# Attention cores: the causal triangle stands in the position bias, not in a matmul of its own

## The reference

```python
sim = jnp.einsum('bhid,bjd->bhij', q, k)            # k: null key, then 1024 keys
bias = jnp.concatenate([null_col, attn_bias], axis=-1)   # attn_bias: [16, 1024, 1024]
sim = sim + bias
neg = -jnp.finfo(sim.dtype).max
causal_mask = jnp.triu(jnp.ones((n, j), dtype=bool), k=j - n + 1)
sim = jnp.where(causal_mask, neg, sim)
sim = jnp.where(mask_p[:, None, None, :], sim, neg)
attn = jax.nn.softmax(sim, axis=-1)
out = jnp.einsum('bhij,bjd->bhid', attn, v)
```

## Time and profile before

| | us |
|---|---|
| median of three runs | 3015.57 |
| span of the profiled execution, first to last instruction | 3060.8 |
| layer 0 attention core (first PE score to the last normalised output) | about 140 to 655 |
| layer 2 attention core | about 1547 to 2069 |
| PE busy, of the span | 2511.8 (82%) |
| DVE busy | 1576.5 (52%) |
| ACT busy | 1325.9 (43%) |
| POOL busy | 938.2 (31%) |

### The profile page before, as it was taken

The page is one execution under the profiler, slowest core; times in us unless marked ns, Lnnn a source line. Parts: engine busy times, 40 slices in busy tenths (PEclk is TensorE's granted clock), DMA queues, the critical chain, the costliest instruction groups (busy, mean ns, idle before and its releaser), DMA issues. The chain is left out here.

```text
span 3060.8 us, 56027 instructions
## 1 busy us (share of the span) xinstructions
PE 2511.8 (82%) x16472; PEld 2054.1 (67%) x16472; DVE 1576.5 (52%) x4371; ACT 1325.9 (43%) x3147; POOL 938.2 (31%) x1172
## 2 busy tenths in 40 slices
PE   5799999988796762995789999998599997673795
PEld 3477777767686752982467777777477786672785
DVE  3366666644214345116766666654588885425111
ACT  2365666653221331333456666664344442152221
POOL 0132333311104454544333333322333430445002
PEclk9999999998897875997989999999799998895898
DMA  7022122202564353521022122210200001144585
GB/s 267 31 78 77 64 86 70 82 27 101 197 230 110 99 193 124 173 65 52 22 85 71 63 86 70 82 42 16 80 1 1 0 0 57 65 157 158 211 307 178
DMA packets 150858, 296.59 MB, mean 97 GB/s; under 512 B 25158, under 2 KB 110406, under 8 KB 144560
## 3 DMA queue, kind: packets, MB, share of 16 engines
q1 hardware_dynamic: 138416, 262.92, 25.5%
q0 software_dynamic: 12288, 31.83, 3.4%
HBM read 240.25 MB, written 64.56 MB: 100 GB/s over the span
## 5 line engine op out<-in xcount | busy, mean ns | idle before, releaser
L796 DVE CUSTOM_DVE_ANT_0 prob_l<-ps_l,bias_l,nsn 128x1024 f32<-128x1024 f32 (+3 forms) x256 | 276.7, 1081 | 112.7 <-DVEq L795 65.4
L796 DVE CUSTOM_DVE_ANT_0 cur_sb<-ps_h,bias_s,nsn 128x128 f32<-128x128 f32 (+3 forms) x256 | 139.7, 546 | 241.7 <-DVEq L795 241.2
L871 ACT ACTIVATE prob_l<-prob_l,nmax 128x1024 f32<-128x1024 f32 (+3 forms) x256 | 252.1, 985 | 1.9 <-DVE nmax L796 1.6
L691 POOL COPY nsn<-nsn 128x4 f32 (+1 forms) x128 | 23.9, 187 | 710.7 <-DVE diff L813 570.5
L727 PE MATMUL ps_l<-khi,stage 128*128 128x512 f32 (+3 forms) x512 | 240.7, 470 | 0.0
L733 PE MATMUL ps_pt<-ident_sb,prob_l 128*128 128x128 f32 x1664 | 231.8, 276 | 5.3 <-ACT cur_sb L855 2.3
L855 ACT ACTIVATE cur_sb<-ps_pt 128x128 f32<-128x128 f32 (+3 forms) x256 | 111.1, 434 | 267.4 <-PE ps_pt L733 267.3
L700 POOL TENSOR_TENSOR stage<-qo,stage 64x256 fp32r<-64x256 f32 x256 | 200.9, 785 | 46.5 <-POOLq L699 46.5
L733 PEld LDWEIGHTS ps_pt<-ident_sb,prob_l 128*128 128x128 f32 x1664 | 186.6, 141 | 29.6 <-ACT cur_sb L855 13.9
L284 PE MATMUL ps_q<-wf,xnT 128*128 128x512 f32 (+1 forms) x384 | 148.2, 539 | 65.5 <-ACT xnT L321 53.5
L2270 POOL TENSOR_TENSOR ss<-simx,sim 128x4096 f32<-128x4096 f32 x16 | 113.4, 7084 | 239.4 <-DVE simx L2419 239.4
(11 more groups left out here) (341 smaller groups left out, 6275.8 us busy)
## 6 DMA issues: line engine op xcount, KB each, us to landing
mlp_ws<-in_L_ffn_experts_dram SPq DMA_DIRECT2D x39, 2052.0 KB, 7.5
xs<-slot_rows SPq DMA_DIRECT2D x156, 128.0 KB, 2.1
slot_outputs<-ys SPq DMA_DIRECT2D x156, 128.0 KB, 1.9
slot_rows<-zero_sb SPq DMA_DIRECT2D x1, 16384.0 KB, 51.9
bias_l<-in_fside_16xSxS_dram SPq DMA_DIRECT2D x16, 512.0 KB, 3.9
mlp_w<-in_L_ffn_experts_dram SPq DMA_DIRECT2D x8, 1024.0 KB
bias_by_partition<-bias_table SPq DMA_DIRECT2D x16, 512.0 KB, 4.2
bias_l<-bias_by_partition SPq DMA_DIRECT2D x16, 512.0 KB, 3.3
```

Source lines behind the costliest of these rows:

```text
L796: dve.tensor_tensor_reduce(out=spans(x, prob), in0=scored(x), in1=spans(x, bias), scale=-1.0, scalar=nsn[:, b, s, h:h + 1], op0=ALU.add, o ...
L871: act.activation(prob[x.s][:, x.h, 0:x.W], prob[x.s][:, x.h, 0:x.W], ACT.Exp, bias=nmax[:, x.b, x.s, x.h:x.h + 1], scale=-1.0, accum_out=r ...
```

## The change

In layer 0 POOL writes -1e38 above the diagonal of the bias tile itself, once it has landed: one `affine_select` of 128x128 for each tile that is loaded (128 of them), in place, and DVE waits for POOL's step instead of the landing. In layer 2 nothing is added: the tail of the table holds -1e38 in place of 0. The mask matmul of every unit is then one, from `km`, over all of its columns. The `dm` buffer and its `affine_select` in `null_phase` go, in both layers.

```diff
@@ null_phase
-        @block.gpsimd
-        def _(gp):
-            gp.wait_ge(masked, 1)
-
-            gp.affine_select(out=att["dm"][:].rearrange("p (m j) -> p m j", j=P),
-                             in_=att["km"][:].rearrange("p b (m j) -> p (b m) j", j=P), compare_op=ALU.is_ge,
-                             fill=MASKED, base=0, pattern=[[0, NT], [-1, P]], channel_multiplier=1).then_inc(triangle, 1)
-            gp.wait_ge(triangle, 1)
@@ core_phase, POOL
-            units(gp, (0, queries))
+            def causal(x):
+
+                if x.b == 0:
+                    block_ = bias[x.s][:, x.h, x.W - P:x.W]
+                    gp.wait_ge(bias_in[x.s][x.h], (x.group + 1) * 16)
+                    gp.sem_inc(gp_b, 1)
+                    gp.affine_select(out=block_, in_=block_, compare_op=ALU.is_ge, fill=MASKED, base=0, pattern=[[-1, P]],
+                                     channel_multiplier=1).then_inc(gp_c[x.s].sem, 1)
+
+            if gp_c:
+                for s in gp_c:
+                    s.open(gp)
+                units(gp, (0, queries), (0, causal))
+            else:
+                units(gp, (0, queries))
@@ core_phase, PE
-                    diagonal = P if hi == W else 0
-                    if hi - lo > diagonal:
-                        pe.matmul(out[:, 0:hi - lo - diagonal], c["ident16"][:], att["km"][:, b, lo:hi - diagonal],
-                                  start=True, stop=False, skip_group_check=True)
-                    if diagonal:
-                        pe.matmul(out[:, hi - lo - P:hi - lo], c["ident16"][:], att["dm"][:, b * S + W - P:b * S + W],
-                                  start=hi - lo == P, stop=False, skip_group_check=True)
+                    pe.matmul(out, c["ident16"][:], att["km"][:, b, lo:hi], start=True, stop=False, skip_group_check=True)
@@ core_phase, DVE
-                    dve.wait_ge(bias_in[s][h], (x.group + 1) * 16)
+                    if gp_c:
+                        dve.wait_ge(gp_c[s].sem, gp_c[s].after("causal", x.group * 4 + h))
+                    else:
+                        dve.wait_ge(bias_in[s][h], (x.group + 1) * 16)
@@ BiasTable.turned_half
-            dve.memset(self.table[:, S:], 0.0).then_inc(self.cleared, 1)
+            dve.memset(self.table[:, S:], MASKED).then_inc(self.cleared, 1)
```

More of the change, by code:

```diff
@@ L503, in null_phase @@
         nrm = ph.sb("nrm", [P, 4])
-        loaded, masked, step, rooted, triangle = (ph.sem() for _ in range(5))
+        loaded, masked, step, rooted = (ph.sem() for _ in range(4))
         block = ph.stack.enter_context(nc.Block())
@@ L590, in core_phase @@
         bias_in = [[ph.sem() for _ in range(4)] for _ in range(2)]
-        sp_b = ph.sem()
+        sp_b, gp_b = ph.sem(), ph.sem()
+        gp_c = [ph.steps("causal") for _ in range(2)] if bias_made is None else None
         gp_s = [ph.steps("null hi0 waited0 lo0 hi1 waited1 lo1") for _ in range(2)]
@@ L2522, in attention_store @@
         "nk": sb("nk", [P, DH]), "nsn": sb("nsn", [P, NT, H]), "nv": sb("nv", [P, DH]), "km": sb("km", [P, B, S], BF16),
-        "dm": sb("dm", [P, B * S], BF16),
     }
```

## The result

| | before | changed |
|---|---|---|
| median, us (20 runs of each) | 3018.49 | 3012.24 |
| span of the profiled execution, us | 3060.8 | 3007.0 |

The ratio is 0.9979 [0.9972, 0.9987]: 6.2 us (0.21%) less, where 14.1 were predicted. The kernel before takes 3018.5 in these runs, not the 3015.57 of the three that the prediction had; 3 of the 10.7 us between 3001.5 and 3012.2 are that.

A forecast was written before the change was run, and what follows sets the result against it. PE was taken to bound both attention cores, with waits for DVE and ACT in every quad. 13.1 us kept, plus 2 from null phases, less 1 for selects, made 14.1: from 3015.6 to 3001.5 us, range 2985 to 3010.

The forecast's parts named there:

- Gross price on PE: Both attention cores: 448 fewer mask matmuls save PE 28.2 us, the upper end if all were on the path.
- The share kept: Quads of both cores: waits for DVE and ACT leave 13.1 us of PE's saving, 6.6 a layer; ends 6 and 28.2.
- Null phases: Before both cores: without the old select, 1 us less in layer 0 and 1 in layer 2; together 2, 0 to 3.
- What the selects cost: Layer 0's core: POOL's 128 selects cost 1 us at its start, between 0 and 3, and nothing in the steady state.
- All on the path: Rival, both cores: DVE and ACT follow the faster PE, all 28.2 us come off, 2986.4 us; chance 0.18.
- columns alone: Rival, both cores: splitting the mask costs PE nothing, so the cores gain nothing, 3014.6 us; chance 0.15.
- selects stop DVE: Rival, layer 0's core: each of 128 selects takes 0.29 us from DVE's chains, 37 us more, 3038.6 us; chance 0.05.

The follow-up runs named there:

- before, again: The kernel before, unchanged, profiled a second time: span 3015.6 us, 478.5 us in each core between first and last long bias load.
- no_select: Changed kernel without POOL's selects in layer 0, DVE waiting for the landing again: ratio 0.9985 [0.9974, 0.9996] to the kernel before.
- light: Kernel before and changed kernel, both with POOL's preparation behind DVE's null-key product, most null-key and normalising work and part of ACT's copy omitted: 2976.63 and 2971.76 us.
- after_again: The changed kernel, nothing further altered, run and profiled once more: median 3012.6 us.

## Why the prediction was wrong

The mechanism was the right one: PE saves, and waits take most of it back. Two things were off. The term "kept" was 13.1 us and is 8.6, and the rest of the program, which the sum put at no change at all, is some 5 us longer.

- **Gross price on PE, 28.2 us: nearly right.** The counts are exact and the halves of p = 0 are equal. Medians of second halves: 512 columns 0.69 (0.75 before), 448 0.60 (0.66), 384 0.53 (0.58), so 0.06, 0.06, 0.05; short units 0.05 to 0.06. At 320 columns I took 0.09; it is 0.06 (0.59 to 0.53 in front of the values), and nothing of it comes through in front of transposes. In all it is about 25 us.
- **The share kept: the step that failed.** Predicted 13.1 us for 32 quads of both layers, 12.3 for 30; the gauge, which spans 30, gives 4.6 and 4.0 = 8.6, about a third of their gross of 24. By p, between neighbouring quads of one p in layer 2: p = 0 keeps about 0.05 us of a quad's time (0.10 predicted), p = 1 0.14 (0.24), p = 2 0.17 (0.30), p = 3 0.13 (0.18). The two waits for DVE's copy at p = 0 grew by 0.01 and 0.10 us, that for DVE's `nmax` at p = 1 by 0.11, that for ACT's copy at p = 3 by 0.06. The prediction counted the units inside the few chains that it had read in single quads. It had no term for the many places where ACT's copy already releases the next transposes (98 of 190 before the change) and PE shows next to no idle time. For p = 2 I said that the saving would make a wait where none was, and still kept 0.30 of 0.52. The place is in PE's rows for its first value matmuls of neighbouring quads, "before, again" and changed: 15.36 and 15.19 us.

```profile
1804.63 1.51 PE L756 MATMUL ps_o<-cur_sb,v 128*64 128x256 f32 x12
1819.99 1.52 PE L756 MATMUL ps_o<-cur_sb,v 128*64 128x256 f32 x12
```

```profile
1795.04 1.51 PE L756 MATMUL ps_o<-cur_sb,v 128*64 128x256 f32 x12
1810.23 1.52 PE L756 MATMUL ps_o<-cur_sb,v 128*64 128x256 f32 x12
```

- **Null phases, 2 us: half at most.** The barrier goes as told: SP's loads begin at 9.78 (13.02 in the earlier trace rows). But ACT waits for them until 18.55 (19.50), and over the profiles this is 18.2 to 19.5 with the change in layer 0 and 18.5 to 19.5 without it: nothing of the 3.2 us is clear of the scatter, as the prediction allowed for full queues. Layer 2's phase falls from 9.28 to 7.94 us, 1.3. Together with the projections behind them about 1 is left in sum, since the projections take longer, by 2 to 3 us in layer 0.

```profile
9.78 0.38 SPq L252 DMA_DIRECT2D w<-in_L_cond_Wq_dram  x1
...
18.55 2.40 ACT L316 ACTIVATE wf<-w,gcol 128x1152 f32<-128x1152 f32 x2 [1.54 <-DMA nb_row<-cond_null_attn_bias_dram]
```

- **What the selects cost, 1 us: nothing, slightly less.** The second quad's preparation stands behind the tiles as described and begins at 147.10, behind the last landing; by the gauge layer 0 still gains 4.6 us where layer 2 gains 4.0.
- **Not in the sum at all:** the untouched rest, some 5 us longer. With 8.6 from the gauge, about 1 from the front and 1 to 2 from the last two quads and the drain (below) the attentions are some 11 us shorter; less 5 is the 6 that is timed. The sum closes, but the 5 are known from single profiles only, and their cause is open. That the drain gave 1 to 2 us to a change that wasn't priced for it is luck.
- **The rivals.** "All on the path" falls by the waits and the gauge, "columns alone" by the equal halves, "selects stop DVE" by `no_select`. What stops DVE is POOL's preparation, which was there before the change.

## To carry to other kernels

Where three engines hand units round in a ring, a saving on the busiest one is worth some fraction of itself, here about a third for 24 us and for 124 us alike (both for the 30 quads of both layers); lightening one waiting chain changed that fraction little (with the moved wait 7.9 us are kept, in the `light` pair 9.4), so calibrate it with one crude run before adding up small terms. A wait that is barely there shows no idle time and still takes a saving: look whether an operation starts right behind the end of another engine's. Look for the stretched copies of an operation (max far above min for one shape): the cheapest gain here was to move a wait so that POOL's reads and a two-input DVE operation don't meet. Compare stretches inside the profile before timed medians, since a change of a few us in one phase is lost in what the others do.

## What the hardware showed

The last two quads of each core and the drain behind them, from the last long bias load to the barrier, take one of several lengths, even for the same kernel: 46.2 us in the changed kernel, 48.8 in `after_again`. The windows of the drain in layer 0 (columns of the earlier trace rows), one of 5.0 and one of 6.9 us, then the value matmuls in it, for the one and the other:

```profile
645.50:650.50 5.00, 3.79 (x33) 2.62 (x35) 1.20 (x4) 1.68 (x3) 0.00 (x0) 1.00 0.01 3
...
648.03 1.95 PE L756 MATMUL ps_o<-cur_sb,v 128*64 128x256 f32 x16
```

```profile
646.10:653.00 6.90, 5.76 (x25) 3.60 (x27) 1.22 (x4) 1.72 (x3) 0.00 (x0) 0.51 0.01 2
...
649.59 3.66 PE L756 MATMUL ps_o<-cur_sb,v 128*64 128x256 f32 x16
```

The same 16 matmuls take 1.95 us at a granted clock of 1.00 and 3.66 at 0.51, the lower of the two levels. Ahead of the fall PE had been waiting for ACT between short groups of transposes, with no scores left to make; but it had done so in the other profile too, where the clock stayed. What decides between them is not shown. It costs 2.6 us in that core. In "before, again" the drain of layer 0 has a mean of 0.76 and that of layer 2 0.72, and both stretches are 48 us long; in most profiles with the change layer 2's is at 46.1, without a fall ahead of the product. That is 1 to 2 us of the measured gain. The matmuls that the change saves don't account for it; whether it shifts the drain so that the clock holds, or by chance, no run isolates.
